# Counting edges into dense blocks: one tile per loop iteration, and out-degrees taken from the count blocks

## The reference

```
t = x @ W.T + b
agg = segment_sum(t[row], col)          # five times in L0 (3), L1, L2
x = layernorm(x + layer(x))
# L3: over all edges
hihj = concat([x[src], x[dst]])
exp_e = exp(silu(bn(hihj @ Wf + bf)));  a = w[src]*exp_e / segment_sum(...)
z = silu(bn(einsum(hihj, Wg) + bg));    h = segment_sum(a * z, dst)
out = bn(h) + x
```

## Time and profile before

| | before |
|---|---|
| median of three runs | 7895.85 us |
| span of the profiled execution | 7903.8 us |
| counting stage, first matmul to the first linear step | 94 to 1535 us |
| first linear step | to 1677 us |
| passes one to four | to 3341 us |
| gather, with most of the sixth pass | to about 6045 us |
| rest | to 7903.8 us |
| busy: TensorE, VectorE, ScalarE, GpSimd | 5452.6, 3716.0, 1419.9, 1922.7 us |

### The profile page before, as it was taken

How to read it: one execution, slowest core, us unless ns; L and a number is a source line. 1 busy time by engine, 2 the same in 40 slices (tenths; PEclk the granted TensorE clock), 3 DMA queues, 4 the chain that set the end, 5 groups by cost and what they waited for, 6 DMA issues and landing times.

```text
span 7903.8 us, 132209 instructions
## 1 busy us (share of the span) xinstructions
PE 5452.6 (69%) x34773; PEld 3268.0 (41%) x34774; DVE 3716.0 (47%) x12527; ACT 1419.9 (18%) x4414; POOL 1922.7 (24%) x3005
## 2 busy tenths in 40 slices
PE   5999999869999999999321211111115899888883
PEld 1333333346666666666100000000002588877773
DVE  8888888733223444455100000000001488888887
ACT  0111233200000000000000000000000176665552
POOL 1222122100000000000577767777774000000000
PEclk8999999879999999999655555555556999999997
DMA  1000111135565656555433333333336555444442
GB/s 40 33 41 41 65 76 78 65 110 191 185 194 187 194 184 194 184 187 182 140 107 107 113 107 109 107 108 108 109 103 146 154 138 129 123 119 114 110 111 59
DMA packets 305154, 958.44 MB, mean 121 GB/s; under 512 B 55676, under 2 KB 124888, under 8 KB 285929
## 3 DMA queue, kind: packets, MB, share of 16 engines
q1 hardware_dynamic: 238729, 741.78, 30.4%
q0 software_dynamic: 66400, 216.36, 10.2%
HBM read 765.85 MB, written 192.08 MB: 121 GB/s over the span
## 4 chain that ended last, share of the span: by engine, by line
PE 48%; another core or an unknown queue 21%; DVE 13%; issue 12%; DVEq 2%; ACT 2%; SPq 1%; DMA 1%; ACTq 0%; POOLq 0%; POOL 0%; PEld 0%; PEldq 0%
PE banks L678 28%; PE banks L637 12%; DVE HSf L1028 3%; PE banks L632 2%; PE banks L627 2%; DVE HSf L1024 1%; DVE HSf L1035 1%; PE banks L668 1%; DVE HSf L1005 1%; PE banks L731 1%; ACT HSf L563 1%; PE banks L738 1%; DVE HSf L1030 1%; ACT AB L518 1%
## 5 line engine op out<-in xcount | busy, mean ns | idle before, releaser
L678 PE MATMUL banks<-HSf,AB 128*128 128x384 bf16 (+2 forms) x14406 | 2727.3, 338 | 1812.8 <-issue 1786.7
L678 PEld LDWEIGHTS banks<-HSf,AB 128*128 128x128 bf16 x14406 | 1417.4, 99 | 3012.7 <-issue 2160.9
L474 POOL DMA_INDIRECT HSf<-table_d,IX x1600 | 1515.0, 947 | 644.0 <-issue 488.6
L903 DVE TENSOR_REDUCE US<-banks 128x128 f32<-128x384 f32 (+1 forms) x294 | 164.1, 558 | 2977.4 <-remote 1738.4
L861 DVE TENSOR_SCALAR T<-T 128x784 bf16<-128x784 f16 x2352 | 985.1, 419 | 224.2 <-PE banks L637 208.1
L637 PE MATMUL banks<-T 128*128 128x392 bf16 x4704 | 965.6, 337 | 3.7 <-DVE T L862 3.0
L637 PEld LDWEIGHTS banks<-T 128*128 128x128 bf16 x4704 | 378.3, 99 | 565.0 <-DVE T L862 380.6
L862 DVE TENSOR_SCALAR T<-T 128x128 bf16<-128x128 f16 x2352 | 581.6, 247 | 0.0
L563 ACT ACTIVATE HSf<-HSf 128x130 f32<-128x130 f32 x1808 | 575.5, 392 | 0.5 <-DVE HSf L1039 0.5
L462 POOL DMA_DIRECT2D table_d<-T x1 | 2.5, 2545 | 2241.1 <-DVE HSf L879 2241.1
L518 ACT ACTIVATE AB<-banks 128x392 f32 x784 | 347.1, 494 | 1102.4 <-PE banks L641 1102.4
(11 more groups left out here) (212 smaller groups left out, 3554.2 us busy)
## 6 DMA issues: line engine op xcount, KB each, us to landing
AB<-counts_d SPq DMA_DIRECT2D x294, 800.0 KB
AB<-counts_d SPq DMA_DIRECT2D x294, 768.0 KB
HSf<-rows_d SPq DMA_DIRECT2D x452, 260.0 KB, 3.1
rows_d<-HSf POOLq DMA_DIRECT2D x100, 1040.0 KB
counts_d<-AB SPq DMA_DIRECT2D x49, 1568.0 KB, 5.2
HSf<-dst_d SPq DMA_DIRECT2D x452, 128.0 KB, 3.4
HSf<-table_d,IX POOLq DMA_INDIRECT x1600
table_d<-T POOLq DMA_DIRECT2D x1, 3185.0 KB, 28.0
```

The source lines that it names most:

```text
L474: g.indirect_dma_start(GS[:, t, :], None, table_d, bass.IndirectOffsetOnAxis(ap=IX[:, t:t + 1], axis=0)).then_inc(g_in[k], 16)
L678: ins = pe.matmul(agg[par][:, 0:wide], AB[:, k, (s - HA * h) * P:(s - HA * h + 1) * P], HS[:, (q - 1) & 1, s, 0:wide], start=(s == 0), sto ...
```

## The change

The counting loop's group becomes one tile (`GW` = 1). GpSimd's loop and `KR` go. VectorE runs the nested loop over windows and tiles itself: it loads the table for four windows, computes the tile number and one of eight slots (`RINGW`), makes `ol` from the tile's low keys and then `oh` with two operations (add the window's key `wcol` to the index row, compare with the edge's key). `oh` and `ol` lie in another buffer with eight slots each. TensorE takes a tile per iteration with slot addresses from registers, and waits for both parts. Four windows have PSUM banks (`WBUF`); a zeroing matmul has one column; the closing matmul goes, and ScalarE waits for the count of used tiles instead, which it reads from `ends`.

The matmuls for out-degrees go. In passes one to four, VectorE sums for each block a quarter of the loaded counts over the destination (`out_degrees`) before it waits for the block's matmuls, and SyncE's loads of these passes wait for that too (`od_read`).

```
-GW = 4
+GW = 1
-SU = 4
-KW = 2 * GW
+RINGW = 8
+WBUF = 4
...
+        oh = HSf[:, 14200:14200 + RINGW * GW * HJ].bitcast(bf16).rearrange("p (k f) -> p k f", k=RINGW * GW)
+        ol = HSf[:, 17400:17400 + RINGW * GW * 64].bitcast(bf16).rearrange("p (k f) -> p k f", k=RINGW * GW)
...   SyncE, load()
+                    if m < 4 and not (isinstance(b, int) and m == 0) or m == 4 and isinstance(b, int):
+                        sp.sem_inc(gate_s, 1)
+                        sp.wait_ge(od_read, m * NB + 2 if isinstance(b, int) else b + (m * NB + 1))
...   GpSimd
-            with g.Fori(0, NW // WU) as w4:
-                e = loads(g, ENG.Pool, tabw, w4 * (4 * WU), 4 * WU - 1, TOPJ * GW)
...
-                        g.tensor_tensor(KR[:, 0, at], KLE[:, 0, ds(t, GW)], nw, ALU.add)
-                        g.tensor_copy(KR[:, 1, at], KLE[:, 1, ds(t, GW)]).then_inc(kr_made, 1)
...   ScalarE
+            with act.Fori(0, NB) as b:
+                e = loads(act, ENG.Activation, ends, b * WPB + 1, WPB, TOPJ)
...
-                    act.wait_ge(window_counted, b * WPB + (k + 1))
+                    act.wait_ge(onehot_used, e[k] + RINGW)
...   TensorE
-            def edges_out(w):
...
+            def window(w, q, j0, j1):
                 pe.wait_ge(window_copied, w + 1)
                 for u in range(2):
-                    pe.matmul(ps[2 * q + u][:, 0:HJ], zz[:, 0:P], zz, start=True, stop=True)
+                    pe.matmul(ps[2 * q + u][:, 0:1], zz[:, 0:P], zz[:, 0:1], start=True, stop=True)
                 with pe.Fori(j0, j1) as j:
+                    pe.wait_ge(lo_made, j + 1)
+                    pe.wait_ge(hi_made, j + 1)
+                    pe.sem_inc(gate_p, 1)
                     for k in range(GW):
-                        pe.wait_ge(onehot_made, j * GW + (k + 1))
+                        at = pe.snap((j & (RINGW - 1)) * GW + k)
                         for u in range(2):
-                            ins = pe.matmul(ps[2 * q + u][:, 0:HJ], ol[:, k, :], oh[:, k, u * HJ:(u + 1) * HJ],
+                            ins = pe.matmul(ps[2 * q + u][:, 0:HJ], ol[:, ds(at, 1), :].rearrange("p a f -> p (a f)"),
+                                            oh[:, ds(at, 1), u * HJ:(u + 1) * HJ].rearrange("p a f -> p (a f)"),
                                             start=False, stop=True, skip_group_check=True)
...   VectorE
+            with v.Fori(0, NW // WU) as g4:
+                e = loads(v, ENG.DVE, tabw, g4 * (4 * WU), 4 * WU - 1, TOPJ * GW)
+                for q in range(WU):
+                    j0, j1, m = e[4 * q:4 * q + 3]
+                    wk = wcol[:, ds(g4 * WU + q, 1)]
+                    with v.Fori(j0, j1) as j:
+                        t = v.snap(tile_at(j * GW - m))
+                        at = v.snap((j & (RINGW - 1)) * GW)
+                        v.wait_ge(onehot_used, j + 1)
+                        for k in range(GW):
+                            ins = ts(ol[:, ds(at + k, 1), :].rearrange("p a f -> p (a f)"), io16[:, 0:P], KLE[:, 1, ds(t + k, 1)], None, ALU.is_equal)
+                        ins.then_inc(lo_made, 1)
+                        for k in range(GW):
+                            ins = ts(oh[:, ds(at + k, 1), :].rearrange("p a f -> p (a f)"), io16, wk, KLE[:, 0, ds(t + k, 1)], ALU.add, ALU.is_equal)
+                        ins.then_inc(hi_made, 1)
...
+            def out_degrees(q, b, par, n):
+                h0, h1 = ((0, 13), (13, HA), (HA, 37), (37, NB))[q - 1]
+                k = 2 * par + (q - 1) // 2
+                at = h0 - HA * ((q - 1) // 2)
+                v.wait_ge(a_in[k], n * 16 + 16)
+                link(v.tensor_reduce(od1[:, 0:h1 - h0], AB[:, k, at * P:(at + h1 - h0) * P].rearrange("p (h d) -> p h d", d=P), AX.X, ALU.add))
+                tt(odeg[:, h0:h1], odeg[:, h0:h1], od1[:, 0:h1 - h0], ALU.add).then_inc(od_read, 1)
...
+                        if 1 <= q <= 4:
+                            out_degrees(q, b, u & 1, i + (q - 1) * 24 if u == 1 else i + ((q - 1) * 25 + 1))
                         partA(q, b, u & 1)
```

More of the change, by code:

```diff
@@ L102, in build @@
         odeg = sb("odeg", [P, NB], f32)
+        od1 = sb("od1", [P, 13], f32)
         tabb = sb("tabb", [1, NB * 4], i32)
@@ L211, in build @@
         misc_copied = sem("misc_copied")
-        onehot_made = sem("onehot_made")
+        lo_made = sem("lo_made")
+        hi_made = sem("hi_made")
         onehot_used = sem("onehot_used")
-        window_counted = sem("window_counted")
+        od_read = sem("od_read")
         window_copied = sem("window_copied")
@@ L614, in _ @@
             pe.transpose(ps[7][0:10, 0:P], wt[:, :], ident[:, :]).then_inc(ranges_turned, 1)
-            pe.sem_inc(onehot_used, KW)
+            pe.sem_inc(onehot_used, RINGW)
             pe.wait_ge(tables_made, 1)
-            def edges_out(w):
[L621 to L627, removed]
@@ L638, in window @@
                                             start=False, stop=True, skip_group_check=True)
[L639 to L643, removed]
+                    ins.then_inc(onehot_used, 1)
             pe.wait_ge(misc_copied, 2)
-            pe.matmul(psO[:, 0:HJ], zz[:, 0:P], zz, start=True, stop=False)
@@ L646, in _ @@
-            e = loads(pe, ENG.PE, ends, 0, WU + 1, TOPJ)
-            for q in range(WU):
-                window(q, q & 1, q - 2 if q >= 2 else None, e[q], e[q + 1])
-            with pe.Fori(1, NW // WU) as w4:
+            with pe.Fori(0, NW // WU) as w4:
                 e = loads(pe, ENG.PE, ends, w4 * WU, WU + 1, TOPJ)
                 for q in range(WU):
-                    window(pe.snap(w4 * WU + q), q & 1, pe.snap((w4 - 1) * WU + (q + 2)), e[q], e[q + 1])
-            pe.wait_ge(window_copied, NW + 2)
@@ L654, in _ @@
-            edges_out(NW - 2)
-            edges_out(NW - 1)
-            pe.matmul(psO[:, 0:HJ], zz[:, 0:P], zz, start=False, stop=True).then_inc(window_counted, 1)
+                    window(pe.snap(w4 * WU + q), q, e[q], e[q + 1])
             def turn(q, b, par):
@@ L682, in mm @@
                         between()
-            pe.wait_ge(misc_copied, 2)
-            pe.wait_ge(window_copied, NW + 2)
+            pe.wait_ge(window_copied, NW + WBUF)
             turn(0, 0, 0)
@@ L825, in _ @@
             link(cp(wi[:, :], wt[:, 5:10]))
-            assert (GW, GM) == (1 << 2, 1 << 3)
-            link(ts(wi[:, 0:4], wi[:, 0:4], 2, None, ALU.logical_shift_right))
+            assert (GW, GM) == (1, 1 << 3)
+            link(ts(wi[:, 0:4], wi[:, 0:4], 0, None, ALU.logical_shift_right))
             link(ts(wi[:, 4:5], wi[:, 4:5], 3, None, ALU.logical_shift_right))
@@ L840, in _ @@
                 link(stt(tab3[:, :, 2], rj1[:, 0:n], float(G), first, ALU.mult, ALU.subtract))
-            lastw = tabw.rearrange("p (n k) -> p n k", k=4)[:, NW - 1, :]
             link(v.memset(tabw.rearrange("p (n k) -> p n k", k=4)[:, :, 3], 0))
-            assert SU == 1 << 2
-            link(cp(rj1[:, 0:1], lastw[:, 1:2]))
-            link(ts(rj1[:, 0:1], rj1[:, 0:1], float(SU - 1), None, ALU.add))
-            link(cp(lastw[:, 3:4], rj1[:, 0:1]))
-            link(ts(lastw[:, 3:4], lastw[:, 3:4], 2, None, ALU.logical_shift_right))
-            link(ts(lastw[:, 1:2], lastw[:, 3:4], 2, None, ALU.logical_shift_left))
             link(v.memset(ends[:, 0:1], 0))
@@ L852, in _ @@
             v.sem_inc(tables_made, 1)
-            bodies, = loads(v, ENG.DVE, tabw, (NW - 1) * 4 + 3, 1, TOPJ)
-            with v.Fori(0, bodies) as i:
-                for s in range(SU):
-                    for k in range(GW):
-                        n = (s & 1) * GW + k
-                        v.wait_ge(onehot_used, i * (SU * GW) + (s * GW + k + 1 + GW))
-                        if k == 0:
-                            v.wait_ge(kr_made, i * SU + (s + 1))
-                        ts(oh[:, k, :], io16, KR[:, 0, n:n + 1], None, ALU.is_equal)
-                        ts(ol[:, k, :], io16[:, 0:P], KR[:, 1, n:n + 1], None, ALU.is_equal).then_inc(onehot_made, 1)
-            v.wait_ge(window_counted, NW + 1)
-            v.tensor_reduce(odeg[:, :], psO[:, 0:HJ].rearrange("p (h d) -> p h d", d=8), AX.X, ALU.add)
+            with v.Fori(0, NW // WU) as g4:
[13 more added lines that the diff above has]
+                        ins.then_inc(hi_made, 1)
+            v.wait_ge(window_copied, NW + WBUF)
             v.wait_ge(rows_in, 16 * 6)
@@ L871, in _ @@
             v.sem_inc(agg_read, 2)
+            v.sem_inc(od_read, 2)
             def split(q, b, t, w):
@@ L959, in _ @@
                 n0 = link.n
+                if 1 <= q <= 4:
+                    out_degrees(q, 0, 0, (q - 1) * 25)
                 partA(q, 0, 0)
```

34 lines of the change are left out of this document (10 added, 24 removed).

## The result

The changed kernel takes 8785.53 us (median of four runs, 8780.52 to 8790.03) against 7895.99 us for the kernel before (four runs beside it, 7892.54 to 7905.39): a ratio of 1.1125, 95% interval 1.1111 to 1.1138. It is 890 us slower. The prediction was 8905 us with a range of 8380 to 9350.

The account below looks back on a forecast made before the run. TensorE's per-tile register work was to bound the counting stage (2450 us against 1441): 7903.8 + 1009 - 3 + 3 = 8913 us of span, 8905 us as median of runs, which lies 8 us lower; range 8380 to 9350.

Parts of the forecast that it names:

- The slower sets the pace. That is TensorE: Counting stage: engines coupled by eight slots; TensorE's 2450 us against 1441 now sets the pace, +1009 us.
- VectorE's price: Counting stage: VectorE's new loop takes 0.90 us per tile (0.80 to 1.0), engine time of 0.50 us beneath it.
- rival A: Counting stage: VectorE is last, TensorE's register work being cheaper; stage 2053 us, +612, total 8508 us; chance 0.25.
- That oh's instruction now does two operations costs nothing: VectorE's one-hot in the counting stage: two shifts over 1664 integers take 1.03 us, as one does.
- TensorE's terms: Counting stage: 1951 tiles at 1.15 us, windows 98 us, table loads 108 us, sum 2450 us.
- B: Counting stage: TensorE's addresses cost more, 1.40 us a tile; stage 2937 us, +1496, total 9391 us; chance 0.18.
- C: Counting stage: register work disappears under the engines, VectorE's 0.50 us sets the pace; -284, 7612 us; chance 0.04.
- A falling clock in this stage costs nothing: Counting stage: TensorE's matmuls, 0.33 us per tile or 0.66 at the lower clock, are hidden under 1.15 us.
- D: Counting stage: around 0.62 us per tile, no change in time; chance 0.01.
- Passes: Passes one to four: some 440 us of added VectorE reductions lie in its idle time, later reloads hidden; 3 us taken.
- Rival E: Passes turn VectorE-bound or wait for late loads: 15 to 60 us on top of whichever other holds; no chance given.
- 0.4 us goes to TensorE's window end: Counting stage before: VectorE's wait of 0.4 us per group for zeroing, odd matmul and out-degree matmuls, removed by the change.

Follow-up runs that it names:

- one_matmul: Changed kernel with zero floors on loop starts, no upper bounds (9612.97 us), now without the right half of each tile's product: 9129.55 us, ratio 1.1558.
- one_matmul_bounded: Changed kernel with zero floors on loop starts, upper bounds kept, without the right one of each tile's two matmuls: 8753.35 us, ratio 1.1091 to the kernel before.
- wide_matmuls: As bounded, but both counting matmuls of a tile 512 columns wide in place of 392, same counts: 7199.39 us, ratio 1.1437 to the kernel before.
- bounded: Changed kernel with a zero floor on values loaded to start loops, upper bounds kept: 7200.9 us beside 6295.61 for the kernel before, on another chip.

## Why the prediction was right, point by point

**What sets the pace.** "The slower sets the pace. That is TensorE" held, by the slots in use and by one_matmul. Its sequencer stands waiting for VectorE in at most two of the 1951 tiles. But the order held by little: the prediction had 400 us between the two engines (2450 and 2053), and there were 40. VectorE's price was the step that failed: 0.90 us per tile taken (0.80 to 1.0 as bounds), 1.07 measured, outside them. The chain shows what made it up: the tile number is a fused record of 0.19 us where a short one of 0.07 was put, and `oh` has two fused records of its own, 0.28 us from `ol` to `oh`. The engine's 0.50 us do lie beneath. The table loads came out lower, (3.02 - 1.07) x 98 = 191 us where 230 were put, and the borders cost it nothing where 67 were put. Its sum was 2053; 1951 x 1.07 + 191 is 2279, and one_matmul_bounded, floors included, has 2297. Had TensorE's terms come out another 2% lower, the mechanism would have been rival A's at nearly the measured time. Rival A at 8508 us was therefore not in reach by its price, even where its mechanism held (one_matmul_bounded, 8753). "That oh's instruction now does two operations costs nothing" is not what the rows show either: `oh` took 419 ns before and takes 483 now (its buffers changed as well, so the cause isn't shown); it costs no time, since the register work is longer.

**TensorE's terms.** Iteration: 1.15 us priced, 1.113 measured, 2171 in place of 2244 us. Its parts fit: counter and branch 0.36 priced and found; wait value and waits 0.28 against 0.25, since both waits share a record; slot 0.10; addresses and dispatch 0.41 against 0.38, with three fused records, not two. Window border: 0.25 us priced, 0.09 measured at 294 borders, so 26 us and not 98. Table load: 1.08 priced, 1.25 measured at 97, 121 us and not 108. Together 2318 against 2450, as the trace has it. So the stage was put 132 us too high. That makes up the 120 us by which 8905 lay above 8785.53, less 6 us by which the old stage was put too high as well (1441 for 1434.5) and 6 us by which the medians moved more than the spans (890 and 884).

**Rivals.** B (1.40 us, a record for each operand) falls: the address of `ol` isn't worked out twice. C (register work disappears under the engines, 0.50 us a tile) falls: the pair took 0.50 us in the flat loop and 1.07 in the nested one. "A falling clock in this stage costs nothing" held: 2340 us at 0.50 and at 0.79, and the same step of a tile at both levels within wide_matmuls. D falls with C.

**Passes.** Held. The reduction, with the columns of the grouped instructions, and the fourth pass as a timeline:

```profile
L924 DVE TENSOR_REDUCE od<-AB 128x12 f32<-128x1536 bf16 (+1 forms) x196 | 349.5, 1783 | 16.3 <-issue 5.5 <-DMA AB<-counts_d 2.7 <-DVE X L860 0.5
```

```profile
3830.44 1.74 DVE L924 TENSOR_REDUCE od<-AB 128x12 f32<-128x1536 bf16 x1
3832.22 0.17 DVE L925 TENSOR_TENSOR odeg<-odeg,od 128x12 f32<-128x12 f32 x1
3832.84 0.56 DVE L871 TENSOR_REDUCE US<-banks 128x128 f32<-128x384 f32 x1 [0.45 <-PE banks L650]
```

It takes 1.74 us, no faster for bf16 than the float rows said (1.75). Of the 2.54 us that L903 waited before, 0.45 are left to its successor L871; the working left 0.19. From 2550 to 4660 us TensorE waits for a load of counts once, 4.3 us at the first pass's start, as before, so the later reloads were hidden too. Rival E falls.

**What the change removes.** "0.4 us goes to TensorE's window end" was credited to four buffers and narrow zeroing together with the out-degree matmuls. The runs split it: the matmuls were 193 us of it, and the buffers with the zeroing 16. So the change as a whole has a half worth about -209 us of stage and, if the two simply add, a half that costs about +1093 (884 + 209); that sum is an estimate.

**What stays open.** VectorE was not made lighter with bounds kept, so no run has the changed kernel with a faster `ol`; since TensorE's sequencer hardly ever stands waiting, it should gain next to nothing. TensorE alone, with VectorE's work gone, wasn't timed. And why VectorE waited 208 us for the out-degree matmuls, 0.49 us a window where 0.33 was expected, wasn't taken apart.

## What to carry to other kernels

Before a loop is made finer, count its sequencer records and not its engine work: here 401 of 2352 pairs went, worth 200 us at 0.50 us each, and with the iterations that this took the stage became 884 us longer. If two engines share a ring of slots, the number of slots in use tells who is last where the lists of waits name both, and so does the time that a sequencer stands at its semaphore record. And split a change that has two halves: the out-degree half alone makes the kernel before 2.4% faster.

## What the runs showed of the hardware that was not expected

A loop's branch, when taken, takes 208 ns on TensorE and 56 ns on VectorE, and the next record starts 0.27 and 0.19 us after its start. Not taken, at a window's end, it takes 76 and 50 ns:

```profile
L613 PEldq COMPARE_BRANCH  x1951: 76/208/239, 96.3 to 2414.3; - x196
L821 DVEq COMPARE_BRANCH  x1951: 50/56/78, 95.2 to 2406.4; - x196
```

The Trainium skill, "Advanced Engine Details and Errata", Control Flow Timing, gives a compare-and-branch about 108 ns and names no engine. This case's traces agree with it on neither engine, and the measurements decide.

Loads of register values differ by engine and count, all on line L300:

```profile
L300 PEldq TENSOR_LOAD <-T x98: 577/584/797, 92.3 to 2403.4; - x98
L300 DVEq TENSOR_LOAD <-T x98: 1534/1543/1809, 92.3 to 2395.4; - x98
...
L300 ACTq TENSOR_LOAD <-T x49: 1962/2122/2235, 92.2 to 2389.0; - x49
```

Five values on TensorE take 0.58 us, fifteen on VectorE 1.54, and eight on ScalarE 2.12.

The same kernel before took 7896 us on one chip and 6296 on another. Little of it can lie in the counting stage, which is 2340 us in bounded on the second chip and 2318 in the changed kernel, without floors, where before takes 7896. In bounded, on the second chip, the sixth pass with the gather beside it runs from 4673 to 5077 us:

```profile
4673.00:5077.00 404.00, 400.27 (x2399) 233.70 (x2400) 132.55 (x384) 0.00 (x0) 284.31 (x317) 0.99 0.86 283
```

In the changed kernel, where before takes 7896, the same 2400 matmuls are spread from 4651 to 7148 us, with a DMA share of 0.41 at 117 GB/s; the pass there waits for something the profile calls another core or an unknown queue. The gather itself takes about as long on both, 2235 us in the changed kernel and 2269 in bounded (first to last of GpSimd's 1600 indirect transfers); on the second chip the attention stage runs beside the rest of it. Why the pass is slow beside the gather on one chip and not on the other wasn't tested. The step from before to the changed program is nearly the same on both: +890 us, and +905 with the floors.
